# Weighting the values of a local attention: two heads of a pair into one 128-row PSUM tile, with zero-padded values

## The reference, cut to what matters

```
h   = shift_token(x);  q, k, v = split(h @ wqkv)          # 8 heads of 64
q   = rotary(l2norm(q) * qs);  k = rotary(l2norm(k) * ksc)
sim = einsum('bhwid,bhwjd->bhwij', bq * 8, bk)            # masked, causal in a window of 128
attn = softmax(sim)
out = einsum('bhwij,bhwjd->bhwid', attn, bv)              # <- the change is in this product
x   = x + out @ wo
```

## Time and profile before

| | |
|---|---|
| median of 3 runs | 2725.2 us (2724.94 to 2728.99) |
| profiled execution, its own time | 2724.97 us |
| its span, first to last instruction | 2723.2 us |
| mean granted TensorE clock | 0.987 |
| DVE, ACT, POOL busy | 71%, 63%, 51% of the span |
| attention of the layers | about 560 to 1250 us and 1640 to 2325 us |
| feed-forward parts | about 1245 to 1642 us and 2320 to 2723 us |

### The profile page before, as it was taken

The page is one execution under the profiler, slowest core; times in us unless marked ns, Lnnn a source line. Parts: engine busy times, 40 slices in busy tenths (PEclk is TensorE's granted clock), DMA queues, the critical chain, the costliest instruction groups (busy, mean ns, idle before and its releaser), DMA issues.

```text
span 2723.2 us, 71565 instructions
## 1 busy us (share of the span) xinstructions
PE 2600.6 (95%) x25088; PEld 2225.9 (82%) x25088; DVE 1931.3 (71%) x3771; ACT 1703.1 (63%) x4184; POOL 1389.7 (51%) x1396
## 2 busy tenths in 40 slices
PE   6999999869999999998999998999999998999998
PEld 4888888747888888886888886888888887788887
DVE  5777777658778787876656556877777777666664
ACT  3666666647778777774444444777777777444442
POOL 7888888567666666662000007666666665000000
PEclk9999999979999999999999999999999999999999
DMA  1111111111111111112111111111111111222221
GB/s 43 37 49 36 44 38 35 37 50 47 41 40 38 37 40 40 40 52 75 51 58 49 56 48 49 39 37 40 40 38 37 40 40 54 70 66 80 80 73 47
DMA packets 165609, 130.30 MB, mean 48 GB/s; under 512 B 23239, under 2 KB 163689, under 8 KB 165462
## 3 DMA queue, kind: packets, MB, share of 16 engines
q1 hardware_dynamic: 163157, 119.80, 14.2%
q0 software_dynamic: 2304, 8.47, 1.1%
HBM read 77.47 MB, written 50.33 MB: 47 GB/s over the span
## 4 chain that ended last, share of the span: by engine, by line
PE 30%; DVE 20%; ACT 20%; issue 6%; SPq 2%; DMA 1%; DVEq 0%; ACTq 0%
ACT attn_E L1036 15%; PE const_banks L1313 6%; PE const_banks L1314 6%; PE const_banks L1315 6%; DVE attn_neg_top L1209 6%; DVE attn_ss L1202 5%; DVE attn_rot_b L1186 5%; ACT attn_sq L1073 5%; PE const_banks L1447 3%; PE const_banks L1449 3%; PE const_banks L1448 3%; SPq L899 2%; DVE attn_E L1164 2%; PE const_banks L1297 1%; DVE attn_rsum L1162 1%
## 5 line engine op out<-in xcount | busy, mean ns | idle before, releaser
L1036 ACT ACTIVATE attn_E<-const_banks,attn_nbias,attn_rn 128x128 f32<-128x128 f32 x1024 | 453.2, 462 | 154.6 <-DVE attn_nbias L1214 154.6
L969 POOL TENSOR_TENSOR attn_qk<-attn_rot_a,attn_rot_b 128x1024 f32<-128x1024 f32 x128 | 303.5, 2371 | 421.8 <-issue 324.4
L956 POOL TENSOR_TENSOR ffn_rstd<-ffn_var,const_neg_half 128x4 f32<-128x4 f32 x32 | 32.3, 1011 | 687.9 <-DVE ffn_var L1139 687.9
L1324 PE MATMUL const_banks<-weights_w_hi,attn_xT_hi 128*128 128x512 f32 x768 | 315.9, 411 | 4.9 <-ACT attn_sq L1073 2.5
L1326 PE MATMUL const_banks<-weights_w_hi,attn_xT_lo 128*128 128x512 f32 x768 | 305.0, 397 | 0.0
L1325 PE MATMUL const_banks<-weights_w_lo,attn_xT_hi 128*128 128x512 f32 x768 | 303.2, 395 | 0.0
L1239 DVE SCALAR_TENSOR_TENSOR ffn_gated<-const_banks,weights_b_col,ffn_gate 128x512 f32<-128x512 f32 (+1 forms) x192 | 143.7, 748 | 215.7 <-ACT ffn_gate L1107 208.6
L1313 PE MATMUL const_banks<-ffn_xT_hi,ffn_w_hi 128*128 128x512 f32 x704 | 283.2, 402 | 6.9 <-DVE ffn_xT_lo L1151 5.4
L1314 PE MATMUL const_banks<-ffn_xT_lo,ffn_w_hi 128*128 128x512 f32 x704 | 280.1, 398 | 0.0
L1315 PE MATMUL const_banks<-ffn_xT_hi,ffn_w_lo 128*128 128x512 f32 x704 | 279.8, 398 | 0.0
L1107 ACT ACTIVATE ffn_gate<-const_banks,weights_b_col 128x512 f32<-128x512 f32 x160 | 110.2, 689 | 227.1 <-PE const_banks L1315 221.7
(11 more groups left out here) (178 smaller groups left out, 7967.4 us busy)
## 6 DMA issues: line engine op xcount, KB each, us to landing
attn_x_res<-xa SPq DMA_DIRECT2D x128, 128.0 KB, 4.7
xb<-attn_x_new SPq DMA_DIRECT2D x128, 128.0 KB, 1.7
ffn_x_<-xb SPq DMA_DIRECT2D x32, 512.0 KB
h<-ident_h SPq DMA_DIRECT2D x64, 128.0 KB, 1.7
xa<-ident_n SPq DMA_DIRECT2D x64, 128.0 KB, 1.7
attn_x_<-xa SPq DMA_DIRECT2D x128, 64.0 KB
xa<-ffn_x_new SPq DMA_DIRECT2D x16, 512.0 KB, 3.6
ffn_add<-h SPq DMA_DIRECT2D x16, 512.0 KB, 6.7
```

The costliest lines, as they stand in the source:

```text
L969: pool.tensor_tensor(qk[:, slot].rearrange("p a n -> p (a n)"), rot_a[:].rearrange("p a h d -> p (a h d)"), rot_b[:].rearrange("p a h d -> ...
L1036: last = act.activation(E[:, r, i], ps_s[:, r, i * P:(i + 1) * P], ACT.Exp, bias=nbias[:, r, i:i + 1], scale=rn[:, slot, h:h + 1], accum_o ...
L1324: pe.matmul(out_, xT_hi[:, slot, k], w.w_hi[:, k, cols], start=(k == 0), stop=False)
```

## The change

The four edits, in words: the tile `v` grows from 4 x 512 to 4 x 4 x 3 x 64 columns, that is three blocks of 64 columns for each pair of heads: values of head 2j, zeros, values of head 2j+1. ACT writes blocks 0 and 2 (L1060), POOL clears block 1 once a layer, at step 0, after waiting for the last output matmul of the feed-forward part before (a wait that stood at step 1). TensorE waits for that (`v_pad`) at step 4. The product takes 128 stationary columns, blocks 0 and 1 for r = 0 ([values, zeros]) and blocks 1 and 2 for r = 1 ([zeros, values]), and both heads add into the same 128 PSUM partitions: `start` at r = 0, `stop` at r = 1. `gate` and `gated` move into the memory that only the feed-forward part uses, over attention tiles.

```diff
-        gate = n.sb("gate", [P, 2, GT])
-        gated = n.sb("gated", [P, 2, GT])
...
-            v = ma.sb("v", [P, 4, INNER])
+            v = ma.sb("v", [P, 4, HEADS // 2, 3, HD])
...
+            gate = mf.sb("gate", [P, 2, GT])
+            gated = mf.sb("gated", [P, 2, GT])
             h_hi = mf.sb("h_hi", [P, 2, FULL, GT], F32R)
...
                 if step is not None and step <= 2 * w.PIECES:
-                    if step == 1:
-                        need(pool, f["out_ps"], layer * ROWS)
                     if step:
                         w.split_forward(pool, layer, (step - 1) // 2, (step - 1) % 2)
                     if step % 2 == 0 and step < 2 * w.PIECES:
                         w.load_forward(pool, layer, step // 2)
+                if step == 0:
+                    need(pool, f["out_ps"], layer * ROWS)
+                    pool.memset(v[:].rearrange("p s j b d -> p (s j) b d")[:, :, 1], 0.0).then_inc(v_pad, 1)
...
-                    act.activation(v[:, (u - 1) % 4], ps_v[:], ACT.Copy).then_inc(s["v_done"], 1)
+                    act.activation(v[:, (u - 1) % 4, :, 0::2], ps_v.rearrange("p (j r d) -> p j r d", r=2, d=HD),
+                                   ACT.Copy).then_inc(s["v_done"], 1)
...
+                    if step == 4:
+                        pe.wait_ge(v_pad, layer + 1)
...
                     for j in range(HEADS // 2):
                         for r in range(2):
-                            h = 2 * j + r
-                            last = pe.matmul(ps_v[r * HD:(r + 1) * HD, j * P:(j + 1) * P],
-                                             v[:, u, h * HD:(h + 1) * HD], ET[:, r, j], start=True, stop=True)
+                            pair = v[:, u, j, r:r + 2].rearrange("p b d -> p (b d)")
+                            last = pe.matmul(ps_v[:, j * P:(j + 1) * P], pair, ET[:, r, j], start=(r == 0),
+                                             stop=(r == 1))
                     last.then_inc(s["o_ps"], 1)
```

More of the change, by code:

```diff
@@ L860, in layers @@
         add_ld = [n.sem("add_ld0"), n.sem("add_ld1")]
-        h_pads, y_pad, y_stored = [n.sem(k) for k in ("h_pads", "x_pad", "stored")]
+        h_pads, y_pad, v_pad, y_stored = [n.sem(k) for k in ("h_pads", "x_pad", "v_pad", "stored")]
         f = {k: n.sem(k) for k in (
```

## The result

The changed kernel takes 2868.84 us (median of 5; 2867.69 to 2876.99) against 2724.94 us of the kernel before (median of 5); the ratio is 1.0529, 95% interval 1.0514 to 1.0545. The forecast was 2820 with a range up to 2842: the direction was right, the size was +144 us where +95 was forecast. The profiled execution is the slowest of the five (2876.99 us, span 2875.2); its rows are set against the kernel before by step, and totals by the medians.

The account below looks back on a forecast made before the run. TensorE was taken as the limit in steady attention. 124 rows at +0.77 us gave +95.5 us, all other terms 0, on 2724.97 us: forecast 2820 us, range 2804 to 2842.

Parts of the forecast that it names:

- The matmuls: TensorE's weighting block L1409: full-width records start every 0.112 us instead of 0.0545, net +0.77 us a row.
- entry: From L1393's last start to L1409's first: 0.20 us becomes one ordinary gap of 0.112, -0.09 us a row.
- exit: From L1409's last start to the next instruction, on a 64 x 64 part: stays at 0.21 us.
- a price for a load of 128 columns: The skill's LDWEIGHTS rule, columns / 1.2: 107 ns for 128 columns, said to agree with L535's 0.112 us.
- The other edits: Copy of v, memset with its wait and v_pad, gate and gated moved: 0 us; bounds 0 to +25 for the copy.
- The other engines' chains don't move against TensorE: What follows L1409 on other engines shifts with TensorE's following work by 0.77 us; nothing shrinks elsewhere.
- gains 0.77 us of slack: Work of other engines started before L1409 was said to gain 0.77 us of slack.
- The number of paying rows: 124 of 128 rows pay 0.77 us each: 109 steady ones and 15 of the other 19; +95.5 us.
- the 109 of the steady stretches: Rows (56 and 53 blocks) where attention runs steadily and TensorE has no idle time, so all pay in full.
- the step is not TensorE's alone: Rival: ScalarE and DVE set the step, hiding the added work; fully hidden 2725 us, 3%; by half 2772, 4%.
- The bare loads: Rival: full-width loads can't overlap the matmul ahead, a record costs up to 0.192 us; 2970 us, 3%.
- the growing copy of v: Rival: ScalarE's copy of v (L1060) grows and gets on the path; up to 2845 us, 5%.

Follow-up runs that it names:

- e8: Kernel before with POOL's L980 waiting for the bias and both heads of a pair writing one column half (half the result left out); 2811.6 us, ratio 1.0302.
- e3: Changed kernel with all edits but the matmuls, which stay the narrow ones of the kernel before; 2728.8 us, ratio 1.0002.
- e12: Kernel before with one of VectorE's two rotary products of a row moved ahead of the second normalisation of E; 2710.01 us, ratio 0.9937.
- e13: Kernel before with the moves of e12 and e9 together; 2705.2 us, ratio 0.9924.
- e1: Changed kernel with one added wait: POOL's scaling of k (L980) waits for VectorE's bias; 2794.8 us, ratio 1.0241.
- e9: Kernel before with ScalarE's copy of v (L1060) and its two waits moved behind the copies of q and k; 2726.11 us, ratio 0.9996.
- e4: Kernel before with its narrow weighting block issued twice, 16 more records a row; 2885.45 us, ratio 1.0575.
- e5: Kernel before with three quarters of its narrow block issued once more, 12 more records a row; 2817.79 us, ratio 1.0329.
- e10: Changed kernel with ScalarE's copy of v moved behind the copies of q and k; 2814.02 us, ratio 1.0316.
- e2: Changed kernel with POOL's last two operations of a row exchanged: the power for q before the scaling of k; 2807.7 us, ratio 1.0288.

## Why the prediction was wrong, step by step

- **The matmuls: right.** Per step, from the starts of TensorE's records: entry 0.202 to 0.109 us (-0.09 as forecast), 15 gaps 0.822 to 1.675 (+0.853; forecast +0.863), exit 0.202 to 0.205. Sum +0.763; forecast +0.77. That a full-width record costs what two halves do side by side was read from L535, and e8 shows why. The prediction also set L535's 0.112 us beside a price for a load of 128 columns; e8 has the same time with loads of 64, so that agreement explains nothing.
- **The other edits: right.** Zero, by e3. The copy of v took 621 ns before and after; the clearing 0.97 and 0.95 us, in POOL's idle time.
- **"The other engines' chains don't move against TensorE ... nothing shrinks elsewhere, as no other engine was the limit": wrong.** This is the step that failed, in two ways.
  - What started before the block "gains 0.77 us of slack" was taken as harmless. But POOL's chain started before it and VectorE's bias after it, and the two had 0.48 us between them. The bias went from 168 to a median of 1009 ns, and 0.66 us of that a step (11.34 against 10.67, means of both layers) reached TensorE: 2868.8 - 2794.8 = 74 us. Neither the forecast nor a rival had it.
  - TensorE was taken as the only limit. Its own work was about 0.155 us a step below a loop of VectorE and ScalarE (0.135 by e12, 0.16 by e13). Of the 0.763 the first 0.155 was free, which leaves 0.61, as e1 has.
- **The number of paying rows: about right in count, and high.** 68 us in e1 over 0.61 us is 112 rows; 124 were counted. If the 109 of the steady stretches all paid, hardly any of the 19 others did, for which 15 were counted. This is worked back from the total, so it is no independent check.
- **The sum as it was:** 68 for the block (e1 against the kernel before; forecast 95.5) plus 74 for the collision (forecast 0) = 142 of 144. Two errors of opposite sign partly covered each other; without the collision the time would have come out 25 us under the forecast, below the range.
- **The rivals.** That the step is not TensorE's alone had been given 3% and 4%, with 40% of the chain of waits over ScalarE and VectorE as the evidence, and was put aside because TensorE's gaps seemed nil. The chain had been right. Records of 0.27 us that start every 0.11 us cover gaps of 0.1 us: the 0.241 us into L1393, against 0.12 without a wait, shows as no idle time. The 0.26 us from the end of q's copy to L1393, which the prediction counted as cover, was the end of that very wait (e9). The bare loads and the growing copy of v were both absent.

The kernel before could have warned of the collision. In the first steps of each layer 16 VectorE instructions with two SBUF inputs are held up like this and take 1.07 to 3.18 us instead of 0.18 or 0.69. One of them, and the sum on POOL that it ends with:

```profile
1694.66 1.66 DVE L1204 TENSOR_TENSOR attn_ssm<-attn_ss,attn_tiny 128x16 f32<-128x16 f32 x1
```

```profile
1693.87 2.41 POOL L969 TENSOR_TENSOR attn_qk<-attn_rot_a,attn_rot_b 128x1024 f32<-128x1024 f32 x1
```

## What to carry to other kernels

A longer or shorter block moves everything behind it against everything that was started ahead of it. List the pairs of VectorE and GpSimd instructions with SBUF inputs that then change order, with the distance between their starts in the trace; where the distance (here 0.48 us) is smaller than the shift, the later one may have to sit out the other's whole instruction, even for an operation of 8 columns. The shift is less than what the block grows by if something in between had slack: the block grew by 0.77 us, and the bias moved 0.53 us against L980 (from 0.48 ahead to 0.05 behind). And before calling an engine the limit, walk the loop of the others once round: if it closes in the time of the step, there are two limits, and both what is added and what is saved on one counts only beyond the other.

## What the runs showed of the hardware that was not expected

- A VectorE multiply of 128 x 8 elements with both inputs in SBUF, started 0.05 us after a POOL multiply of 128 x 512, ended with it: 1.02 us for 0.17. In the changed kernel, e4, e5 and e10 every bias that started inside L980, bar one that came as it ended, did so: 97, 112, 43 and 55 rows.
- The same instruction was not held up by POOL's power of 128 x 8 elements, though that runs 1.64 us and reads SBUF too: in e2 it started 0.29 us into it and took 0.17 us, and in the kernel before 1.25 us into L975. Nor was the normalising of E (128 x 512, two SBUF inputs): in the kernel before 121 of them started inside the power L982 and took 0.69 us as elsewhere. The page named above has the first of the two keep the interface for its whole instruction, and names no exception; where it and these rows differ, the rows decide. What sets the power apart wasn't tried.
- Plain fp32 records with 128 moving columns start every 0.112 us on the full array. When two column halves alternate they start in pairs 0.007 us apart, one pair every 0.109 us, so 0.0545 us each on the mean. When the same narrow records stay in one half they start every 0.109 us, after a first gap of 0.16 (e8). The width of the load made no difference.
